# A graph layer on one core: GpSimd issues its row gathers without a small fill after each

## The reference

```python
xn = layernorm(x)
feat = (xn @ W_n).reshape(N, 8, 32)
el, er = einsum(feat, attn_l), einsum(feat, attn_r)          # one row of 32 numbers per node each
e = leaky(((el[src] + er[dst] + em) * mask).sum(t) / 3)      # per edge and head
a = softmax of e over the edges that share dst
gnn = segment_sum(feat[src] * a, dst)                        # feat[src]: one table row per edge
mix = layernorm(linear_attention(xn) @ Wout) * gamma
x = x + gnn + mix
x = x + sum over 8 experts of w_x * (relu(bn(relu(bn(LN(x) @ W1))@ W2)) @ Wo + bo)
```

## Time and profile before

| | us |
|---|---|
| median of 3 runs | 3161.24 (3158.49 to 3166.12) |
| the profiled execution, its own time | 3170.54 |
| its span, first to last instruction | 3168.9 |

### The profile page before, as it was taken

One profiled execution on the slowest core, in us unless ns is written; L12 is line 12 of the kernel. 1 busy time (PEld: TensorE's weight loads), 2 busy tenths in 40 slices (PEclk: granted clock), 3 DMA queues, 4 the chain that ended last, 5 costly groups with the idle time before them and its releaser, 6 DMA issues. The chain is left out here.

```text
span 3168.9 us, 76579 instructions
## 1 busy us (share of the span) xinstructions
PE 2874.6 (91%) x21350; PEld 2376.5 (75%) x21351; DVE 2638.7 (83%) x4799; ACT 1700.9 (54%) x5754; POOL 1852.1 (58%) x3341
## 2 busy tenths in 40 slices
PE   8996589998999999999899999898599999999999
PEld 5565377776777777777777777776388888888899
DVE  5676698998999998899999999898587777777776
ACT  5552256665666665666666666665543333333343
POOL 3888688888888888888888888887000000000000
PEclk9998899999999999999999999999799999999999
DMA  8678867676776767676667676665211000000000
GB/s 312 211 252 298 307 193 202 202 208 197 206 212 199 208 195 197 199 206 199 203 196 205 199 207 206 199 203 156 76 52 34 21 22 21 22 21 18 18 23 10
DMA packets 275943, 500.38 MB, mean 158 GB/s; under 512 B 80679, under 2 KB 177474, under 8 KB 269008
## 3 DMA queue, kind: packets, MB, share of 16 engines
q0 software_dynamic: 85456, 282.69, 30.8%
q1 hardware_dynamic: 190336, 215.88, 21.4%
HBM read 410.81 MB, written 87.57 MB: 157 GB/s over the span
## 5 line engine op out<-in xcount | busy, mean ns | idle before, releaser
L972 POOL DMA_INDIRECT gat<-scratch_table,idx x1360 | 1323.6, 973 | 239.0 <-issue 229.9
L1325 PE MATMUL ps_s<-msg,oh 128*128 128x272 f32 x4000 | 1029.0, 406 | 106.0 <-ACT tmp L1038 55.9
L1325 PEld LDWEIGHTS ps_s<-msg,oh 128*128 128x128 f32 x4000 | 742.7, 193 | 255.5 <-ACT tmp L1038 107.6
L1047 ACT ACTIVATE acc<-acc,sc 128x33 f32<-128x33 f32 x2000 | 458.8, 340 | 224.2 <-DVE acc L1161 222.3
L1610 ACT ACTIVATE h<-ps_h,fsh,fsc 128x512 f32<-128x512 f32 (+1 forms) x416 | 291.1, 751 | 508.8 <-PE ps_h L1824 508.8
L1173 DVE TENSOR_TENSOR msg<-gat,ps_m 128x2048 f32<-128x2048 f32 x250 | 559.3, 2277 | 0.0
L1563 POOL DMA_DIRECT2D out<-y x13 | 9.9, 759 | 897.2 <-DVE y L1778 897.2
L1038 ACT ACTIVATE tmp<-ps_s,sc 128x33 f32<-128x33 f32 x2000 | 386.7, 305 | 17.2
L1027 ACT CAST oh<-ps_o 128x1024 f32<-128x1024 bf16 x250 | 259.3, 1037 | 139.2 <-PE ps_o L1264 137.7
L1653 DVE CAST h_hi<-h 128x1024 fp32r<-128x1024 f32 (+1 forms) x208 | 137.2, 660 | 201.9 <-ACT h L1610 201.8
L1186 DVE TENSOR_TENSOR_SCAN runm<-penr,ps_e 16x1024 f32<-16x1024 bf16 x125 | 284.3, 2274 | 12.8
(11 more groups left out here) (224 smaller groups left out, 5319.8 us busy)
## 6 DMA issues: line engine op xcount, KB each, us to landing
d16r<-scratch_dst SPq DMA_DIRECT2D x250, 256.0 KB
scratch_acc<-acc SPq DMA_DIRECT2D x250, 136.0 KB
scratch_ahead<-stage SPq DMA_DIRECT2D x26, 1152.0 KB, 4.8
gat<-scratch_ahead POOLq DMA_DIRECT2D x26, 1152.0 KB
edge<-in_edge SPq DMA_DIRECT2D x250, 88.0 KB
gat<-scratch_table,idx POOLq DMA_INDIRECT x1360
scratch_table<-stage POOLq DMA_DIRECT2D x49, 144.0 KB, 5.3
xq<-in_xT SPq DMA_DIRECT2D x7, 896.0 KB, 11.4
```

Source lines behind the costliest of these rows:

```text
L972: pool.indirect_dma_start(out=gat[:, s, c, :], out_offset=None, in_=scr["table_rows"], in_offset=bass.IndirectOffsetOnAxis(ap=rows[:, at:a ...
L1047: act.mul(acc[:, new, cols], acc[:, old, cols], sc[:, j, 0, h:h + 1]).then_inc(scaled, 1)
L1325: last = pe.matmul(ps_s[j][:, 0:SUMS], oh[:, s, j, c, :], msg[:, 2 * (s % 2) + j, c, :], start=(c == 0), stop=(c == C - 1), skip_group_che ...
```

## The change

The fills are taken out, in both stages. The class `Rests`, its three constants, the two tiles `rest_n` and `rest_e` and the semaphore `g_rested` go with them. Nothing else is changed: the same DMAs in the same order.

```diff
-REST_AFTER = 1
-RESTS = 1
-REST_WIDTH = 16
...
-class Rests:
-    def __init__(self, tile, rested, n):
-        self.tile, self.rested, self.n = tile, rested, n
-
-    def after(self, pool, c):
-        if c % REST_AFTER != REST_AFTER - 1:
-            return
-        for _ in range(RESTS):
-            if self.n:
-                pool.wait_ge(self.rested, self.n)
-            pool.memset(self.tile[:, :], 0.0).then_inc(self.rested, 1)
-            self.n += 1
...
-        rest = sb("rest_n", [P, REST_WIDTH])
...
-            rests = Rests(rest, made, READY + 1)
...
                     ).then_inc(staged[i % 2], 16)
-                    rests.after(pool, c)
...
-        rest = sb("rest_e", [P, REST_WIDTH])
...
-        rested = sem("g_rested")
...
-            rests = Rests(rest, rested, 0)
...
                 ).then_inc(gathered[s], 16)
-                rests.after(pool, c)
```

## The result

| | before | after |
|---|---|---|
| median, us | 3161.78 (3158.49 to 3166.12, 4 runs) | 3137.73 (3135.92 to 3143.26, 4 runs) |
| ratio | | 0.9927, 95% interval 0.9914 to 0.9940 |
| span of the profiled execution | 3168.9 | 3135.7 |

The change makes the kernel 24 us, 0.73%, faster. 31 us slower was forecast; the measured time lies in the stated range only because that range, 3079 to 3360, holds both signs. Five more runs of the same kernel on another chip gave 3138.08 us and again 0.9927 (0.9914 to 0.9941).

The account below looks back on a forecast made before the run. GpSimd's unbroken gathers were taken to bound the edge stage. +28 us there and +3 in the node stage made +31: 3201.5 us for the profiled execution, 3192 for the median; range 3079 to 3360.

Parts of the forecast that it names:

- Where the bound is: Edge stage: GpSimd runs without a pause and sets the stage's end; each nanosecond more per gather costs 1.4 us.
- the reserve: Edge stage: VectorE's steps of 14.1 us leave 82 us that can be gained before VectorE sets the pace.
- The fill's reported time isn't to be had: Edge stage: the fills' own 203.7 us were not counted as gain; by durations -82, by spacing +31.
- lies inside a gap of 0.30 that is there anyway: Ahead of each gather: the fill's 0.13 us was said to be hidden within a 0.30 us gap.
- a gap that is 0.12 shorter: Ahead of a gather behind a fill: idle 0.18 us, against 0.30 behind a plain load.
- I take 1.28 us, that is +0.02 a gather: Gather spacing without fills, from gathers behind plain loads, against 1.26 with a fill: +28 us in the edge stage.
- The row for the lower bound: Plain loads every 0.535 us, 0.66 behind gather and fill: the fill's 0.13 us simply goes, gathers 1.13 us apart.
- The rival of much dearer gathers in a row: Both stages: a gather behind a gather takes 1.38 us, +0.12, giving 3354 us; chance 0.22.
- The mask operations: Edge stage: delays beside VectorE's masks, about 21 us of GpSimd's time, were expected to stay and fall on the gathers.
- The node stage: +3 us predicted: Node stage: 208 gathers ahead at +0.02 us, +4.2, delay SyncE's stores some 1.5 us past VectorE's end; taken as +3.
- Simply gained: Rival, edge stage: gathers 1.13 us apart free 183 us, capped at 54 to 82 by the reserve, 3095 us; chance 0.25.
- nothing: Rival: the gap of 0.30 swallows the fill, gathers stay 1.26 us apart, 3161 us; chance 0.13.

Follow-up runs that it names:

- seven_gathers: Changed kernel without fills, the last of each edge group's 8 gathers made a plain DMA of the same size: 3082.75 us, 0.9753 of the kernel before.
- two_fills: Kernel before with two fills behind each gather, the second waiting on the first: 3667.0 us, ratio 1.1589.
- wide_fill: Kernel before with each fill 128 x 128 instead of 128 x 16: 3283.15 us, ratio 1.0390.
- fill_after_load: Changed kernel without fills, but one fill of 128 x 16 behind each of the edge stage's 26 plain loads: 3134.84 us, 0.9917 of the kernel before.
- fills_edge_only: Kernel before with the node stage's 208 fills removed and the edge stage's 1408 kept: 3164.71 us, ratio 1.0000.

## Why the prediction was wrong

**Where the bound is: right.** GpSimd, at 58% of the span, sets the edge stage. What its stretch of gathers gains or loses the kernel gains or loses, nearly one for one (29.7 us of the 33.2 between the profiled spans, and the 496.7 and 113.0 us of the two dearer fills), and the reserve held: from the kernel before to `seven_gathers` 77 us were gained where I had 82.

**The fill's reported time isn't to be had: right.** Of 203.7 us in the edge stage 29.7 came back, and the gap of 0.30 "issue" ahead of each gather stands as foreseen. But the reason given, that the fill "lies inside a gap of 0.30 that is there anyway", was wrong: `two_fills` and `wide_fill` show fill and gather in series. That the price came out near zero is an offset of 0.13 by 0.12 us, which the prediction had seen as "a gap that is 0.12 shorter" and not explained.

**The step that failed** is "I take 1.28 us, that is +0.02 a gather". It took the gather behind a plain load as the stand-in for a gather behind a gather. Measured is 1.25, -0.01. That row mixed two things, the absence of a fill and the presence of a load; `fill_after_load` separates them, and the load is what makes it longer. With a price near zero the sign hangs on the hundredth of a microsecond, and 1408 x 0.03 us between 1.28 and 1.25 are 42 of the 55 us by which the sum was off. The row for the lower bound had the same fault: 0.535 us is a plain DMA behind a plain DMA, behind a gather it is 0.60, so the fill cost the load 0.06 us and not 0.13. The rival of much dearer gathers in a row (+0.12, from the same load) falls with it.

**The mask operations: right to leave them in the sum.** Intervals between gathers with a mask operation in them lost 20.9 us over the commonest interval before and 18.0 after, so all but 3 of the 21 us stayed, now in the gathers alone. The rest of the 11 us (7 + 4 above) isn't the masks': the intervals over by more than 0.6 us, 8 before and 4 after, have no mask in them, and the others without a mask lost 8.7 us before and 4.9 after. What these were is open.

**The node stage: +3 us predicted, nothing measured.** The term was a price of +0.02 a gather too, and falls with it: the commonest spacing of the gathers ahead is 1.25 us without fills. The profile has its SyncE store at 351.85 instead of 356.25, but `fills_edge_only` gives 1.0000.

**The rivals.** "Simply gained" had the sign but not the mechanism: gathers are 1.25 us apart and not 1.13, and 24 us of the 54 to 82 came. Of the four cases "nothing" was nearest in spacing, and its window of 0.0045 us was right: 0.01 us was enough to leave it. The chance for faster had been 0.25, and all of it on a gain to the reserve; a small gain from a gather 0.01 us quicker was in none of the cases.

## What to carry to other kernels

An engine's share of the span hides a stage that it sets: look whether it ever pauses, and who waits for it at the end. The price of a small instruction between two long ones is the spacing with it less the spacing without it, and a row with another neighbour is no measure of it to a hundredth of a microsecond, which 1400 repetitions turn into 14 us. Be wary of an instruction that waits on the one issued just before it in the same queue: with such a wait, and one tile for both, a second fill cost 503 us, without them 26.

## What the runs showed of the hardware

- From the end of one gather to the end of the next: 1.25 us with nothing or a no-op between, 1.26 with a fill of 128 x 16, 1.28 with two that don't wait for each other, 1.33 with one of 128 x 128, 1.39 with two of which the second waits for the first (the commonest spacing in each kernel).
- Gathers that overlap a VectorE mask of 0.49 us take 1.03 us on average, the others 0.95; about a quarter of them are over 1.1 us, with a mean of 1.20. Beside the form with two tensor inputs, 1.23 us long, the mean is 1.33 and the longest 2.00.
- Four gathers of padding at the end of the stage cost 13.9 us between medians, not only the 5.0 of their issue: another 4 to 5 us lay between the last gather and TensorE's start.
